# Gathers of the next pair's second sequence spread over the heads' loop, and their additions moved later, in a two-layer decoder

## The reference

```python
# end of layer 0: each token adds up six rows of the experts' output
yk = out[slot].reshape(T, K, H)                      # K = TOP_K = 6
y = jnp.sum(yk * topk_w[..., None], axis=1)
# layer 1: mixer, then attention with 8 heads over the feature axis
x = x + _L1_attn_ref(_layernorm(x), ...)
x = x + _L1_xattn_ref(_layernorm(x), ctx_2048, ctx_2048, gamma)
# in it: qk = einsum('bhdq,bhdl->bhql'), 512 x 512 scores a head
sm = jax.nn.softmax(qk, axis=-1)
ret = jnp.einsum('bhql,bhdl->bhdq', sm, vh)
```

## Time and profile before

| | us |
|---|---|
| median of 3 runs | 3235.02 |
| lowest, highest | 3234.54, 3240.52 |
| profiled execution: span | 3302.3 |
| profiled execution: own time | at least its span; what lies around it is not recorded |
| TensorE busy | 3036.6 (92%) |
| VectorE busy | 2340.6 (71%) |
| ScalarE busy | 1598.7 (48%) |
| GpSimd busy | 804.8 (24%) |

### The profile page before, as it was taken

One profiled execution on the slowest core, in us unless ns is written; L12 is line 12 of the kernel. 1 busy time (PEld: TensorE's weight loads), 2 busy tenths in 40 slices (PEclk: granted clock), 3 DMA queues, 4 the chain that ended last, 5 costly groups with the idle time before them and its releaser, 6 DMA issues. The chain is left out here.

```text
span 3302.3 us, 61057 instructions
## 1 busy us (share of the span) xinstructions
PE 3036.6 (92%) x22689; PEld 2436.3 (74%) x22689; DVE 2340.6 (71%) x4406; ACT 1598.7 (48%) x3657; POOL 804.8 (24%) x968
## 2 busy tenths in 40 slices
PE   7999999997998799999999958898999989999999
PEld 5666666664887688888888846666767678888888
DVE  5666666664775588888888666778786777777776
ACT  3323333342221455555555426556566766555555
POOL 1221122122554111111111053242422112222222
PEclk9999999998998899999999969899999989999999
DMA  6314233221111577777777631212111032222222
GB/s 262 128 67 178 110 128 105 113 103 40 36 50 33 187 240 246 250 243 241 241 242 248 229 96 65 69 42 72 58 59 33 8 117 85 74 76 75 74 74 71
DMA packets 144969, 401.85 MB, mean 122 GB/s; under 512 B 39200, under 2 KB 47904, under 8 KB 131824
## 3 DMA queue, kind: packets, MB, share of 16 engines
q1 hardware_dynamic: 106320, 323.30, 28.7%
q0 software_dynamic: 18976, 50.45, 5.2%
q10 hardware_dynamic: 19456, 25.18, 2.2%
HBM read 344.09 MB, written 54.76 MB: 121 GB/s over the span
## 5 line engine op out<-in xcount | busy, mean ns | idle before, releaser
L1465 POOL DMA_INDIRECT xg<-normed_rows,idx x128 | 125.0, 977 | 668.8 <-PE psum L1547 590.2
L2685 POOL TENSOR_TENSOR mixf<-act 128x256 f32<-128x256 f32 x128 | 143.7, 1123 | 470.7 <-DVE act L2969 470.7
L174 POOL TENSOR_SCALAR ve<-mv 128x1 f32<-128x1 f32 x112 | 36.9, 330 | 853.0 <-DVE mv L774 587.9
L1562 PE MATMUL psum<-xT_hi,wgu_hi 128*128 128x192 f32 (+1 forms) x1536 | 228.5, 271 | 4.2 <-ACT aT_lo L1529 4.2
L1562 PE MATMUL psum<-xT_lo,wgu_hi 128*128 128x192 f32 (+1 forms) x1536 | 223.3, 268 | 0.0
L1562 PE MATMUL psum<-xT_hi,wgu_lo 128*128 128x192 f32 (+1 forms) x1536 | 222.5, 267 | 0.0
L1601 DVE TENSOR_TENSOR wgu_lo<-wgu,wgu_hi 128x1408 fp32r<-128x1408 f32 x128 | 202.6, 1624 | 22.6 <-ACT wgu_hi L1489 22.4
L1562 PEld LDWEIGHTS psum<-xT_hi,wgu_hi 128*128 128x128 f32 (+1 forms) x1536 | 190.6, 182 | 28.8 <-ACT wgu_hi L1489 21.5
L1502 ACT ACTIVATE eth<-psum 128x192 f32<-128x192 f32 (+1 forms) x192 | 63.4, 330 | 297.9 <-PE psum L1562 294.9
L2030 ACT ACTIVATE scratch<-psum,smin 128x512 f32<-128x512 f32 x256 | 173.9, 686 | 63.3 <-DVE smin L2427 59.9
L2427 DVE TENSOR_REDUCE smin<-psum 128x2 f32<-128x1024 f32 x128 | 155.5, 1217 | 66.5 <-PE psum L2184 41.1
(11 more groups left out here) (438 smaller groups left out, 8593.3 us busy)
## 6 DMA issues: line engine op xcount, KB each, us to landing
wgu<-in_w_gu_dram SPq DMA_DIRECT2D x64, 1408.0 KB, 6.0
w_slot<-w_split SPq DMA_DIRECT2D x21, 2048.0 KB
wd<-in_w_d_dram SPq DMA_DIRECT2D x64, 512.0 KB, 8.6
w_raw<-in_w_dram SPq DMA_DIRECT2D x128, 256.0 KB, 2.6
expert_out<-yo ACTq DMA_DIRECT2D x64, 256.0 KB, 5.2
w_slot<-w_split SPq DMA_DIRECT2D x28, 512.0 KB
wd<-in_w_d_dram SPq DMA_DIRECT2D x64, 192.0 KB, 9.0
w_split<-w_slot SPq DMA_DIRECT2D x4, 2048.0 KB
```

The lines of the kernel that those rows point to most:

```text
L1465: pool.indirect_dma_start(out=xg[b][0:w, t, :], out_offset=None, in_=rows, in_offset=bass.IndirectOffsetOnAxis(ap=idx[b][0:w, t:t + 1], ax ...
L1562: ins = pe.matmul(bank(2 + m)[0:w, gu * CAP:(gu + 1) * CAP], wgu2[b][wp][:, gu, kc, m0:m0 + w], xT2[b][xp][:, kc, :], start=(i == 0 and kc ...
L2685: pool.tensor_tensor(mixf[:, g % LAG, :], act2[:, g % LAG, 0, :], act2[:, g % LAG, 1, :], ALU.add).then_inc(sy["f_mix"], 1)
```

## The change

GpSimd's wait for gather i of `second + 2` becomes `smin_ready >= 32p + 7 + 3i // 2` for p = 1 and 2: gathers 0 to 11 wait for minima 6, 7, 9, 10, 12, 13, 15, 16, 18, 19, 21 and 22. On VectorE the additions of tile 0 go from steps 12 to 17 to steps 16 to 21, those of tile 1 from one in each of steps 18 to 23 to two in each of steps 25, 26 and 27. The first pair's loop is as before.

```diff
--- before.py
+++ after.py
@@ -1907,7 +1907,7 @@
                 context_low(second)
                 if more:
                     for i in range(GATHERS if p else 2 * GATHERS + 2):
-                        pool.wait_ge(sy["smin_ready"], HP * p + i + 1)
+                        pool.wait_ge(sy["smin_ready"], HP * p + (7 + 3 * i // 2 if p else i + 1))
                         if p:
                             gather(second + 2, i)
                         elif i < GATHERS:
@@ -2532,8 +2532,11 @@
                     if more:
                         if p == 0 and 12 <= i < 12 + GATHERS:
                             combine(first + 2, (i - 12) // TOPK, (i - 12) % TOPK)
-                        if p and 12 <= i < 12 + GATHERS:
-                            combine(second + 2, (i - 12) // TOPK, (i - 12) % TOPK)
+                        if p and 16 <= i < 16 + TOPK:
+                            combine(second + 2, 0, i - 16)
+                        if p and 25 <= i < 28:
+                            combine(second + 2, 1, 2 * (i - 25))
+                            combine(second + 2, 1, 2 * (i - 25) + 1)
                         if p == 0 and 24 <= i < 24 + 6:
                             combine(second + 2, 0, i - 24)
                         if p == 0 and 30 <= i < 33:
```

## The result

The change made the kernel slower: 3247.06 us median of 6 runs (3242.41 to 3252.95) against 3235.18 of the kernel before (6 runs, 3234.21 to 3240.52), ratio 1.0031 with a 95% interval of 1.0021 to 1.0041, or +11.9 us. The forecast was 3237.6.

What follows compares the result with a forecast made beforehand. VectorE and TensorE were taken as level in the heads' loop, with TensorE's pauses beside gathers likely only in the trace. Additions' terms sum to +1.3 us a pair, +2.6 for two: 3235.0 + 2.6 = 3237.6 us, range 3218 to 3242.

Steps and rivals of the forecast that it cites:

- Step 27's pair falls into slack: Step 27's two additions mostly fit VectorE's 1.22 us idle before minimum 29 in step 28: +0.2 us a pair.
- 13 to 15: Steps losing one addition each: TensorE's 6.78 us becomes the limit instead of 8.50, −1.7 us a pair.
- 16 to 21: Steps 16 to 18 enter with TensorE no longer ahead, +0.5 us a pair; steps 19 to 21 as before.
- 22 to 24: Additions leave steps 22 and 23, −1.0 us a pair; step 24 becomes TensorE's, +0.4.
- 25, 26: Two dependent additions in each step, where VectorE already sets the pace: +2.9 us a pair.
- I put the recording somewhat ahead.: TensorE's pauses beside back-to-back gathers judged likelier a cost of profiling than real, on the trace's own length.
- Case A: Pauses beside gathers exist only in the trace; only the additions count: 3237.6 us, chance 0.48.
- The 67.3 us: Profiled span over the unprofiled median, read as at least that much trace time absent from the timed runs.
- Case B: Pauses beside gathers in the second and third pair are real and go: 3220.0 us, chance 0.30.
- still go together: Gathers 0 and 1 find minima 6 and 7 done or nearly done when `context_low` ends, so both go together.
- Case D: Slower: steps 25 and 26 pay in full, TensorE keeps its old pace in 13 to 15, 22 to 24: 3241.2 us, chance 0.12.
- a span of 3287.3: Whole profiled execution after the change: 3302.3 − 17.6 + 2.6 us, whether or not the timed runs share the pauses.

Runs made afterwards that it cites:

- e5: Changed kernel with TensorE repeating scores in its waits of steps 27 and 28; 3289.35 us, ratio 0.9963 to the kernel before on the same chip.
- e1: The kernel before, unchanged, profiled once more; span 3240.2 us, loops of the second and third pair 82.4 us each.
- e9: Kernel before with gathers two in three steps from minimum 1 on and additions in VectorE's idle time; 3300.65 us, ratio 0.9967.
- e13: Kernel before with one gather a step from minimum 7, additions one a step in 14 to 23, two in 28; 3290.82 us, ratio 0.9944.
- e3: Changed kernel without doubled additions: one gather a step from step 7, single additions in 16 to 27; 3242.92 us, ratio 1.0015 to the kernel before.
- e4: Changed kernel with TensorE repeating scores behind both halves of step 28's turning; 3242.96 us, ratio 1.0017 to the kernel before.
- e11: Same kernel as e5, run on another chip; 3293.51 us, ratio 0.9949 to the kernel before there.
- e10: The changed kernel, unchanged, on a chip where TensorE pauses; 3299.61 us, ratio 0.9963 to the kernel before there.

## Why the prediction was wrong

It failed in two places.

**"Step 27's pair falls into slack", and the sum that ends with it.** The terms, by step times. Those with "clock kept" are e5's second pair, where the change's additions ran at clock 1.00, with the repeated scores in TensorE's idle time:

| steps, second pair | before (e1) | after | clock kept | forecast | after − e1 | clock kept − e1 |
|---|---|---|---|---|---|---|
| 13 to 15 | 8.50 | 6.91 | 6.92 | −1.7 | −1.6 | −1.6 |
| 16 to 21 | 16.28 | 16.78 | 16.97 | +0.5 | +0.5 | +0.7 |
| 22 to 24 | 7.33 | 6.93 | 6.92 | −0.6 | −0.4 | −0.4 |
| 25, 26 | 5.30 | 8.24 | 8.24 | +2.9 | +2.9 | +2.9 |
| 27, 28 | 6.20 | 7.47 | 6.18 | +0.2 | +1.3 | 0.0 |
| 29, 30 | 6.04 | 8.06 | 6.01 | 0 | +2.0 | 0.0 |
| sum | | | | +1.3 | +4.7 | +1.6 |

Each term that is VectorE's or TensorE's pace was right to 0.2 us, the slack of step 28 included: with the clock kept it takes all of step 27's pair. What the sum lacks is the clock: it put steps 29 and 30 at nothing, and they cost 2.0 us, with 1.3 in step 28. The same idle time of TensorE that made the slack look free let its clock fall: 3.2 us in this pair (87.1 against 83.9), 3.8 in the third (87.8 against 84.0). Two pairs: 2 × 1.6 + 7.0 = 10.2 of the 11.9 us. The rest is inside the interval (6.8 to 13.3 us). I had read the same sequence, idle and then half the clock, in the earlier trace rows, and had counted it only as something that the change removes.

**"I put the recording somewhat ahead."** Case A was right that the pauses are absent in the runs that are judged, and its reason was wrong. No run shows anything lost by recording: own time is span + 1.7 us in the profile after, and on the chips with pauses the kernel before takes 3302 to 3310 us in the median of runs without a profile. The 67.3 us are about the distance between those medians and the 3235 to 3239 us of the others. The first trace of before has the pauses and the span of the one kind and the times beside it are of the other; its own time and its chip are not recorded, so that it ran on another chip than the timed runs is inferred. "NOTIFIC — the notification-queue block" of the Trainium skill, section "Overflow: three behaviours, one of which stalls the engine", says that records can push back and throttle an engine. No run shows such a stall. "Runtime: NRT & Kernel Launch" of the Trainium skill, section "The ~15µs preamble/postamble breakdown", puts the profile's total about 6.2 us above the execution's time. The span used here, first to last instruction, is another measure and lies 1.7 us below the execution's time.

**Case B**, that the pauses are real and go, holds for the second and third pair on chips III and IV, where the changed kernel was run: it is 10.6 and 12.5 us faster there, where B had −15.0. Of the pauses' 17.6 us all went (minimum 9 comes after 0.83 us of idle time); the clock took about 7 back. That a run of gathers behind one another is what TensorE pauses beside was right: e9 against e13 shows it. That gathers 0 and 1 "still go together" was not: gather 1 waited for minimum 7 and went 2.4 us behind gather 0.

**Case D**, the slower one, named the place next to the right one and the wrong mechanism. Steps 13 to 15 and 22 to 24 gave back what I expected, and steps 25 and 26 cost what I expected; a price of 6.2 us by additions not returned did not occur.

The other statements: the first 12 steps at 28.6 to 30 us, right (28.6); steps 13 to 31 longer by 1 to 1.6 us, wrong (4.7 by e1); no wait for gathered rows, right, all 12 additions follow their predecessor with no idle time put down to a landing; a span of 3287.3, wrong, since the profile came from the other kind of chip.

## What to carry to other kernels

Work that is moved into an engine's slack can still cost something when TensorE idles beside it and its granted clock then falls: look for what TensorE must catch up on directly behind the place, and read the granted clock there. Where a trace shows TensorE pausing beside runs of indirect DMAs, issue them one at a time between steps, and check at which step the issuing engine comes free, or the waits do nothing. When the profile's span and the timed runs are far apart, consider that the two may come from different chips before you blame the profiler, and profile the same kernel a second time.

## What the runs showed of the hardware

- The same kernel takes 3235 to 3239 us on two sets of runs and 3303 to 3310 on four, each of the five numbered sets on a chip of its own. In the slower kind TensorE has gaps in issue beside runs of indirect DMAs (busy 3.92 of 8 us beside gathers, 4.56 beside scatters); in the quicker it has none beside the same runs (8.00 of 8 both times, at 298 and 4 GB/s). What differs in the chips no run shows.
- There, nine gathers 1.25 us apart cost 7.3 us in one step, six cost 3.4 there and, by a granted clock of 0.58, 3.1 two steps on; gathers 1.8 us apart or more cost nothing (e13).
- The order of instructions does not settle whether the clock falls: pairs with the same instructions differ by 3.3 to 3.6 us (e3, e4), and the unchanged first pair took 85.0 us in one execution and 87.5 in another on the same chip. Behind three doubled steps it fell in 8 pairs of 8 (TensorE busy for 2.90 and 3.23 of 6 us in the two pairs of the changed kernel). Work that computes nothing new, 1 us at a time in TensorE's waits, made the kernel 6.1 us faster on chip III (e11 against e10).
